# Transposing the query and key stacks by DMA in a token-mixing, attention and expert layer

## The chip, the cores and the metric

The kernel runs on one core of one Trainium2 chip. The metric is the device time of one execution in microseconds. The kernel before took 2010.56 us (median of 3 runs, 2005.82 to 2010.73).

## The reference

The input x has 8 batches of 512 tokens, with 256 entries of 4 taps each. A transformer layer of width 256 follows, all in float32:

```
h = einsum('bhid,oi,od->bho', x, weighted_sum, weight)       # mixing: 1024 inputs to 256
n = layernorm(h)
q, k, v = split(n @ qkv_w.T + qkv_b)                          # 16 heads of 16
q, k = unit(rotate(q)), unit(rotate(k))                       # rotary, then length 1
a = softmax(q @ k.T / 4) @ v                                  # 512 x 512 per head
h = h + a @ out_w.T + out_b
n = layernorm(h)
w = sigmoid(n @ Wg + bg), zero where it is not over 0.5       # 8 experts, dense
h = h + sum_e w[:, e] * (relu(n @ W1[e] + b1[e]) @ W2[e] + b2[e])   # 256 -> 1024 -> 256
```

## The kernel before

**Work.** Every float32 product is made of parts: a high part, and a low part that holds the rest. An expert product is three float16 matmuls (high by high, high by low, low by high). Each batch has 64 chunks (8 experts of 8 hidden tiles of 128). For a chunk, "f1" is the first layer (six matmuls of 512 columns into bank_h, L850), then ScalarE makes two relus of it (L657, float32, and L660, float16 high part), GpSimd makes the low part (L540), and "f2" is the second layer (twelve matmuls of 256 columns into bank_f, L869 to L872), three chunks later. After the eighth chunk of an expert VectorE adds the result to the sum ("acc", L1073), for which the next expert's f2 waits. There are two banks for f1, so TensorE starts f1 of chunk c only when the relus of chunk c - 2 are done.

**Order.** The order of the work is written out by hand. `attention_order()` gives each step of the next batch's mixing and attention a place in units of chunks of this batch's expert work, and `bodies()` merges the two lists into one. Each engine walks through the same merged list, in order, and takes from each step its own part. So what an engine waits for holds up all that stands behind it in the list. A step with a fraction below .5 stands between f1 and f2 of its chunk, otherwise behind f2. The first batch's attention runs alone, in an order of its own (`alone`), with four banks for the scores; there is no expert work beside it. During the experts of batch 0 the float16 parts of the weights are made ("maxima", "scales", "parts") and stored in HBM, later batches load them again.

**Steps of the attention that the change touches.** "split" makes the high part xh (ScalarE) and the low part xl (VectorE) of a tile of x; "mix" is the mixing product of a tile of 128 tokens (L683 to L685); "ln1" the layernorm; "ln1_turn", "qkv" and "rotate" the projection and the rotary step of a tile; "qk_norm 0" and "1" the reciprocal lengths of two tiles; "unit" scales query and key of a tile (L987). "stack" writes both, with their parts, into one float16 buffer `stack`: for the query (high, low, high, low), for the key (high, high, low, low), 16 heads of 64 columns, 1024 in all; ScalarE writes the high half, VectorE the low half (L996). "qk_turn" has TensorE transpose the 2 x 8 blocks of 128 x 128 (L752) into banks bank_s (bank_f in the first batch), and ScalarE copies them to `qt` and `kt`. There is one `stack`, so tile t + 1 waits for the turn of tile t. "scores" need all four tiles of qt and kt. At "qkv 3" GpSimd adds the output bias to the residual (L560).

**SyncE** issues all DMAs, in order, all on one queue. For each expert it waits until the slot is free and loads w1 and w2 (1 MB each). Tile t of x goes into one of two buffers, free when tile t - 2 is split. The result of a batch is stored behind the last expert.

Of the kernel before, what the change touches and what calls it, by code (L numbers as in the profile page):

```python
# [26 lines left out]
P = 128  # L27
# [28 lines left out]
def attention_order(alone=False):  # L56


    steps = []
    for t in range(TT):  # L60
        steps += [(MIX[t - 1] - 0.05 if t else 0.3, "split", t), (MIX[t], "mix", t),
                  (9.0 + 1.5 * t, "ln1_turn", t), (10.55 + 1.5 * t, "qkv", t), (10.6 + 1.5 * t, "rotate", t),
                  (17.1 + 1.5 * t, "unit", t), (18.6 + 1.5 * t, "stack", t), (20 + 1.5 * t, "qk_turn", t)]
    steps += [(6.8, "ln1", 0), (14.7, "qk_norm", 0), (19.2, "qk_norm", 1)]
    if alone:

        order = ["ln1_turn 0", "ln1_turn 1", "qkv 0", "rotate 0", "ln1_turn 2", "qkv 1", "rotate 1", "qk_norm 0",
                 "unit 0", "ln1_turn 3", "qkv 2", "stack 0", "rotate 2", "unit 1", "qkv 3", "qk_turn 0", "stack 1",
                 "rotate 3", "qk_norm 1", "qk_turn 1", "unit 2", "stack 2", "unit 3", "qk_turn 2", "stack 3",
                 "qk_turn 3"]  # L70
        places = {name: 8 + 0.1 * k for k, name in enumerate(order)}
        steps = [(places.get(f"{stage} {n}", at), stage, n) for at, stage, n in steps]
    first = 25.6
    for n in range(2 * UNITS):
        steps.append((first + PACE * n, "scores", n))
    for u in range(UNITS):
        steps.append((first + PACE * (2 * u + 3) + 0.1, "weigh", u))
    for g in range(GROUPS):
        steps += [(first + PACE * (8 * (g + 1) + 1) + 0.15, "out_copy", g),
                  (first + PACE * (8 * (g + 1) + 3) + 0.2, "out_turn", g)]  # L80
    tail = first + PACE * (2 * UNITS + 4) + 1
    for t in range(TT):
        steps += [(tail + t, "att_turn", t), (tail + t + 1.1, "project", t), (tail + 7.6 + 0.8 * t, "ln2_turn", t),
                  (tail + 8.5 + 0.8 * t, "logits", t)]
    steps += [(tail + 5.2, "ln2", 0), (tail + 11.2, "gates", 0), (tail + 12.7, "gates_turn", 0),
              (tail + 13.7, "bias2", 0)]
    steps.sort(key=lambda s: s[0])
    return steps


PACE = 0.66
MIX = [2.1, 3.5, 4.9, 6.3]
PIECES = 4


# [97 lines left out]
def build(nc, x_t, mix_w, mix_sum_t, qkv_w_t, qkv_b, out_w_t, out_b, gate_w, gate_b, w1, b1_t, w2, b2,  # L193
# [5 lines left out]
    with ExitStack() as ctx:  # L199
# [11 lines left out]


        ident = sb("ident", [P, P])
        ident16 = sb("ident16", [P, P], F16)
        mix = sb("mix", [P, 2, XK, D], F32R)
        qkvw = sb("qkvw", [P, 2, DK, QKV], F32R)
        outw = sb("outw", [P, 2, DK, D], F32R)
# [113 lines left out]
        qk_unit = signal("qk_unit", TT)  # L331
        stack_hi = signal("stack_hi", 2 * TT)
        stack_ready = signal("stack_ready", 2 * TT)
        stack_turned = signal("stack_turned", 2 * TT)
        qt_out = signal("qt_out", TT)
        kt_out = signal("kt_out", TT)
        scored = signal("scored", 4 * UNITS)
        exped = signal("exped", 4 * UNITS)
        weighed = signal("weighed", UNITS)
# [36 lines left out]
        def qkv_banks(t, alone):  # L376

            return bank_h if alone and t % 2 else bank_s

        def qk_turn_bank(a, alone):  # L380

            return (bank_f if alone else bank_s)[a][:, :].bitcast(F16).rearrange("p (h t) -> p h t", t=P)

        def stack_slots(t, a):

# [50 lines left out]
        def _(sp):  # L436
# [43 lines left out]
            def load_expert(b, e):  # L480


                s = e % 2
                wait(sp, z_ready, b, HM * (e - 1))
                sp.dma_start(w1s[s][:], w1_parts[e]).then_inc(w1_in[s].sem, 16)
                wait(sp, f2_done, b, HM * (e - 1))
                sp.dma_start(w2s[s][:], w2_parts[e]).then_inc(w2_in[s].sem, 16)

            def store(b):
                for half in range(2):  # L490
# [4 lines left out]

            load_raw(0)
            load_x(1, [0, 1])
            load_raw(1)
            store_parts(0)
            load_x(1, [2, 3])  # L500
            load_raw(2)
            store_parts(1)
            for e in range(2, EXPERTS):
                if e + 1 < EXPERTS:
                    load_raw(e + 1)
                store_parts(e)
# [3 lines left out]
            load_x(2, [0, 1])  # L510
            load_expert(1, 0)
            load_expert(1, 1)
            store(0)

            def body(b, more, far):
                if more:
                    load_x(b + 1, [2, 3])
                for e in range(2, EXPERTS):
                    load_expert(b, e)
                if far:  # L520
                    load_x(b + 2, [0, 1])
                if more:
                    load_expert(b + 1, 0)
                    load_expert(b + 1, 1)
                store(b)

            for i in range(1, BATCHES - 2):
# [6 lines left out]
        def _(pool):  # L534
            def steps(stage, n, fb, ab):
# [15 lines left out]
                elif stage == "reduce":  # L551

                    pool.wait_ge(maxima, 3 * (n + 1))
                    if n:
                        pool.wait_ge(scales, n)
                    pool.partition_all_reduce(mxr[:], mx[:], P, bass.bass_isa.ReduceOp.max).then_inc(maxima_all, 1)
                elif stage == "qkv" and n == TT - 1:

                    wait(pool, ln1_out, ab, TT)
                    pool.tensor_tensor(resid[:], resid[:], outb[:].unsqueeze(1).broadcast_to([P, TT, D]),  # L560
                                       ALU.add).then_inc(resid_biased.sem, 1)
# [1 line left out]
            make_mix(pool, 1)  # L563
            pool.memset(v1[:, :, :, 1, :], 1.0).then_inc(pool_consts, 1)
            pool.wait_ge(consts_in, 16 * 9)
            pool.tensor_copy(ident16[:], ident[:]).then_inc(pool_consts, 1)
            run(pool, steps)

        @block.scalar
        def _(act):  # L570
            def copy(out_ap, in_ap):
                return act.activation(out_ap, in_ap, ACT.Copy)  # L572

            def take_turned(t, a, b, alone):

                dst, done = ((qt, qt_out), (kt, kt_out))[a]
                wait(act, stack_turned, b, 2 * t + a + 1)
                wait(act, scored, b, 0)
                copy(dst[:, :, t * P:(t + 1) * P], qk_turn_bank(a, alone)).then_inc(done.sem, 1)

            def split_x(b, t):

# [6 lines left out]
            def steps(stage, n, fb, ab):  # L589
# [20 lines left out]
                elif stage == "stack":  # L610
                    wait(act, qk_unit, ab, n + 1)
                    for a in range(2):
                        wait(act, stack_turned, ab, 2 * (n - 1) + a + 1)
                        high, _, unit_qk = stack_slots(n, a)
                        copy(high, unit_qk).then_inc(stack_hi.sem, 1)
                        if n:
                            take_turned(n - 1, a, ab, fb is None)
                elif stage == "qk_turn" and n == TT - 1:
                    for a in range(2):
                        take_turned(n, a, ab, fb is None)  # L620
                elif stage == "scores":
                    u, half = divmod(n, 2)
                    if half == 0:
# [53 lines left out]
        def _(pe):  # L677
# [17 lines left out]
            def steps(stage, n, fb, ab):  # L695
# [27 lines left out]
                elif stage == "qkv":  # L723
# [18 lines left out]
                elif stage == "qk_turn":  # L742
                    if fb is not None:
                        wait(pe, qkv_out, ab, 2 * TT)
                    if n == 0 and fb is None:
                        pe.wait_ge(pool_consts, 2)
                    for a in range(2):
                        wait(pe, stack_ready, ab, 2 * n + a + 1)
                        wait(pe, (qt_out, kt_out)[a], ab, n)
                        turned = qk_turn_bank(a, fb is None)  # L750
                        for h in range(HEADS // 2):
                            last = pe.transpose(turned[:, h, :],  # L752
                                                stack[:, a, 2 * h:2 * h + 2, :, :].rearrange("p h s d -> p (h s d)"),
                                                ident16[:])
                        last.then_inc(stack_turned.sem, 1)
                elif stage == "scores":
                    (g, tile), half = divmod(n // 2, TT), n % 2
                    if n == 0:
                        wait(pe, qt_out, ab, TT)
                        wait(pe, kt_out, ab, TT)  # L760
                        wait(pe, qkv_out, ab, 2 * TT)
                    for j in range(2):
                        h = 4 * g + 2 * half + j
# [5 lines left out]
                elif stage == "weigh":  # L769
                    g, tile = divmod(n, TT)  # L770
                    wait(pe, exped, ab, 4 * (n + 1))
                    if n == 0:
                        wait(pe, qkv_out, ab, 2 * TT)
                        wait(pe, ln1_lo, ab, TT)
                    if tile == 0:
                        wait(pe, o_out, ab, g)
                    for j in range(4):
# [103 lines left out]
        def _(dve):  # L881
# [23 lines left out]
            def steps(stage, n, fb, ab):  # L905
# [76 lines left out]
                elif stage == "unit":  # L982

                    wait(dve, weighed, ab, 0)
                    scale = y1[:, n * 2 * HEADS:(n + 1) * 2 * HEADS].unsqueeze(2)\
                        .broadcast_to([P, 2 * HEADS, HD])
                    dve.tensor_tensor(units_at[:, n % 2, :].rearrange("p (h d) -> p h d", d=HD),  # L987
# [2 lines left out]
                elif stage == "stack":  # L990
                    wait(dve, qk_unit, ab, n + 1)
                    for a in range(2):
                        high, low, unit_qk = stack_slots(n, a)
                        wait(dve, stack_hi, ab, 2 * n + a + 1)
                        wait(dve, stack_turned, ab, 2 * (n - 1) + a + 1)
# [182 lines left out]
```

## Time and profile before

| | |
|---|---|
| median of 3 runs | 2010.56 us |
| profiled execution | 2008.53 us, of it span 2006.6 us, mean granted clock 0.975 |
| TensorE busy | 1907.4 us (95%), 13152 matmuls |
| ScalarE, VectorE, GpSimd busy | 57%, 39%, 34% |
| DMA queue of SyncE | 174.52 MB, 24.8% of 16 engines |
| costliest group | L850, first expert layer, 754.8 us in 3072 matmuls |

Starts and durations are in microseconds from the start of the span. The duration of a matmul holds its way through the array: matmuls that follow one another overlap, and what one costs is the distance from its start to the next one's. "[0.40 <-DVE xl]" behind an instruction is the time for which its engine was idle before it and what ended that. PE is TensorE, ACT ScalarE, DVE VectorE, POOL GpSimd, SP SyncE. DMA issues have the time from the issue to the landing.

### The profile page before, as it was taken

How to read it: one execution, taken by the hardware profiler on the slowest of the kernel's cores; microseconds unless marked ns; L12 is line 12 of the kernel's file. 1: busy time of each engine (PE TensorE's matmuls, PEld its weight loads, DVE VectorE, ACT ScalarE, POOL GpSimd, SP SyncE). 2: the span in 40 equal slices, each digit the busy share in tenths (PEclk: the TensorE clock that was granted, in tenths of full speed). 3: DMA queues.
4: the chain of work that ended last, by engine and by line, in shares of the span. 5: the costliest groups of instructions: out<-in, count | busy, mean ns of one | idle time of the engine just before them, and what ended most of it. 6: DMA issues, size and time to landing. Idle time of an engine off the chain costs nothing.

```text
span 2006.6 us, 33214 instructions
## 1 busy us (share of the span) xinstructions
PE 1907.4 (95%) x13152; PEld 1210.5 (60%) x13152; DVE 776.4 (39%) x1636; ACT 1143.0 (57%) x1969; POOL 676.7 (34%) x570
## 2 busy tenths in 40 slices
PE   5679898899999999999999999999999999999999
PEld 4246543576547764577646775467645776466666
DVE  6656933538103470145502372034800455022000
ACT  2654676544774467644765447754576447654444
POOL 1102422335223343333423353233433334233443
PEclk8779999999999999999999999999999999999999
DMA  4013232332112311231212221133211322113221
GB/s 156 31 57 113 104 138 84 126 138 84 64 64 106 115 64 64 79 125 63 83 64 105 97 84 64 64 106 97 83 64 64 124 77 85 64 64 116 101 89 53
DMA packets 40442, 176.64 MB, mean 88 GB/s; under 512 B 4056, under 2 KB 17120, under 8 KB 23904
## 3 DMA queue, kind: packets, MB, share of 16 engines
q1 hardware_dynamic: 40288, 174.52, 24.8%
q8 instruction: 105, 1.72, 0.3%
q14 instruction: 49, 0.40, 0.1%
HBM read 153.54 MB, written 20.97 MB: 87 GB/s over the span
## 4 chain that ended last, share of the span: by engine, by line
PE 78%; DVE 8%; issue 6%; ACT 1%; POOL 1%; POOLq 0%; DVEq 0%; ACTq 0%
PE bank_h L850 28%; PE bank_f L869 10%; PE bank_f L871 10%; PE bank_f L872 10%; PE bank_o L779 5%; PE bank_s L767 3%; PE bank_s L683 2%; PE bank_s L685 2%; PE bank_s L684 2%; PE bank_s L752 1%; DVE qk L972 1%; DVE tmp_b L967 1%; DVE y L890 1%; POOL hl L540 1%; PE bank_s L833 1%
## 5 line engine op out<-in xcount | busy, mean ns | idle before, releaser
L540 POOL TENSOR_TENSOR hl<-h,hh 128x512 f16<-128x512 f32 x512 | 608.2, 1188 | 1131.8 <-ACT hh L660 724.9
L850 PE MATMUL bank_h<-x,w1s 128*128 128x512 f16 x3072 | 754.8, 383 | 9.0 <-ACT hh L660 8.6
L657 ACT ACTIVATE h<-bank_h,b1s 128x512 f32<-128x512 f32 x512 | 353.6, 691 | 453.3 <-PE bank_h L850 438.3
L869 PE MATMUL bank_f<-w2s,hh 128*128 128x256 f16 x2048 | 562.3, 275 | 2.1 <-DVE acc L1073 1.6
L871 PE MATMUL bank_f<-w2s,hh 128*128 128x256 f16 x2048 | 560.5, 274 | 0.0
L872 PE MATMUL bank_f<-w2s,hl 128*128 128x256 f16 x2048 | 560.4, 274 | 0.0
L850 PEld LDWEIGHTS bank_h<-x,w1s 128*128 128x128 f16 x3072 | 288.2, 99 | 333.9 <-issue 43.5
L660 ACT ACTIVATE hh<-bank_h,b1s 128x512 f16<-128x512 f32 x512 | 352.6, 689 | 0.0
L627 ACT ACTIVATE probs<-bank_s 128x512 f32<-128x512 f32 x480 | 262.4, 604 | 154.6 <-PE bank_s L767 154.2
L869 PEld LDWEIGHTS bank_f<-w2s,hh 128*128 128x128 f16 x2048 | 201.9, 99 | 112.5 <-issue 43.0
L1073 DVE SCALAR_TENSOR_TENSOR acc<-bank_f,gw,acc 128x256 f32<-128x256 f32 x256 | 106.1, 477 | 364.0 <-PE bank_f L872 363.9
L871 PEld LDWEIGHTS bank_f<-w2s,hh 128*128 128x128 f16 x2048 | 201.3, 98 | 48.1 <-issue 0.3
L872 PEld LDWEIGHTS bank_f<-w2s,hl 128*128 128x128 f16 x2048 | 201.2, 98 | 24.1
L1000 DVE RECIPROCAL rc<-bank_m 128x16 f32<-128x16 f32 x32 | 8.2, 258 | 400.0 <-PE bank_m L789 400.0
L779 PE MATMUL bank_o<-probs,v 128*32 128x512 f32 x1024 | 138.1, 612 | 1.2 <-ACT tmp_b L572 0.6
L767 PE MATMUL bank_s<-qt,kt 64*128 64x512 f16 x480 | 99.2, 393 | 13.0 <-ACT probs L627 11.8
L683 PE MATMUL bank_s<-mix,xh 128*128 128x256 f32 x256 | 77.9, 304 | 15.9 <-DVE xl L913 15.9
L767 PEld LDWEIGHTS bank_s<-qt,kt 64*128 64x128 f16 x480 | 24.6, 93 | 100.0 <-issue 49.7
L609 ACT ACTIVATE probs<-qk 128x512 f32<-128x512 f32 x32 | 20.2, 630 | 102.9 <-DVE qk L954 102.9
L913 DVE TENSOR_TENSOR xl<-xraw,xh 128x512 fp32r<-128x512 f32 x64 | 47.7, 757 | 76.0 <-ACT xh L572 63.6
L684 PE MATMUL bank_s<-mix,xh 128*128 128x256 f32 x256 | 73.7, 288 | 0.0
L685 PE MATMUL bank_s<-mix,xl 128*128 128x256 f32 x256 | 73.5, 287 | 0.0
(134 smaller groups left out, 1736.0 us busy)
## 6 DMA issues: line engine op xcount, KB each, us to landing
w1s<-w_parts SPq DMA_DIRECT2D x56, 1024.0 KB, 4.8
w2s<-w_parts SPq DMA_DIRECT2D x56, 1024.0 KB, 4.8
xraw<-in_x_t_dram SPq DMA_DIRECT2D x32, 512.0 KB, 4.8
raw<-in_w_dram SPq DMA_DIRECT2D x16, 1024.0 KB, 6.7
w_parts<-w1s SPq DMA_DIRECT2D x8, 1024.0 KB, 8.8
w_parts<-w2s SPq DMA_DIRECT2D x8, 1024.0 KB, 10.7
out_dram<-acc SPq DMA_DIRECT2D x16, 256.0 KB, 6.1
raw<-in_qkv_w_t_dram SPq DMA_DIRECT2D x1, 768.0 KB, 7.2
```

Source lines behind the costliest of these rows:

```text
L540: pool.tensor_tensor(hl[n % HBUFS][:], h32[n % 2][:], hh[n % HBUFS][:], ALU.subtract)\
L627: act.activation(probs[u % 2][:, 2 * half + j, :], score_bank(2 * n + j, fb is None)[:, :], ACT.Exp, scale=SCORE_SCALE).then_inc(exped.sem, 1)
L657: act.activation(h32[n % 2][:], bank_h[n % 2][:, :], ACT.Relu, bias=b1s[:, e, m:m + 1]).then_inc(h_hi.sem, 1)
L660: act.activation(hh[n % HBUFS][:], bank_h[n % 2][:, :], ACT.Relu, bias=b1s[:, e, m:m + 1]).then_inc(h_hi.sem, 1)
L683: pe.matmul(out_ap, high[k], w[k], start=start and k == 0, stop=False, skip_group_check=True)
L684: pe.matmul(out_ap, high[k], lo_w[k], start=False, stop=False, skip_group_check=True)
L767: pe.matmul(score_bank(2 * n + j, fb is None)[:, :], kt[lo:lo + 64, h // 2, tile * P:(tile + 1) * P], qt[lo:lo + 64, h // 2, :], start=Tru ...
L779: last = pe.matmul(bank_o[32 * j:32 * j + 32, :], v1[:, tile, h, :, :].rearrange("p s d -> p (s d)"), probs[n % 2][:, j, :], start=(tile = ...
L850: last = pe.matmul(bank_h[n % 2][:, :], w[:, wp, k, m * P:(m + 1) * P], x16s[fb % 2][:, xp, k, :], start=(k == 0 and wp + xp == 0), stop=( ...
L869: pe.matmul(o, high, w[:, 0, m, :], start=(m == 0 and t % 2 == 0), stop=False, skip_group_check=True)
L871: pe.matmul(o, high, w[:, 1, m, :], start=False, stop=False, skip_group_check=True)
L872: last = pe.matmul(o, low, w[:, 0, m, :], start=False, stop=(m == HM - 1), skip_group_check=True)
```

## The change

TensorE's transposes of the stacks, their banks' use, ScalarE's copies to qt and kt and the step "qk_turn" are gone. SyncE issues two transposing DMAs per tile instead (`turn_stacks`), each 128 x 1024 in float16, from `stack` to the tile's columns of qt or kt. ScalarE's and VectorE's parts of "stack" now wait for the landing of the tile before; "scores" wait for the landing of all. The places move: mixing, layernorm and projection come 1.1 chunks earlier, unit 0 is at 15.2 instead of 17.1, and units 1 to 3 at 17.9, 19.2 and 20.5 instead of 18.6, 20.1 and 21.6; each stack is 1.4 behind its unit. Scores begin at 25.6 as before. The output bias is added at 23.7. On SyncE, the first tile's transposes stand between the loads of w1 and w2 of expert 3, the others behind them; tiles 2 and 3 of x are asked for before the store of the batch instead of behind it.

```
-                  (9.0 + 1.5 * t, "ln1_turn", t), (10.55 + 1.5 * t, "qkv", t), (10.6 + 1.5 * t, "rotate", t),
-                  (17.1 + 1.5 * t, "unit", t), (18.6 + 1.5 * t, "stack", t), (20 + 1.5 * t, "qk_turn", t)]
-    steps += [(6.8, "ln1", 0), (14.7, "qk_norm", 0), (19.2, "qk_norm", 1)]
+                  (7.9 + 1.5 * t, "ln1_turn", t), (9.45 + 1.5 * t, "qkv", t), (9.5 + 1.5 * t, "rotate", t),
+                  (UNIT[t], "unit", t), (UNIT[t] + 1.4, "stack", t)]
+    steps += [(5.7, "ln1", 0), (12.9, "qk_norm", 0), (15.7, "qk_norm", 1), (23.7, "out_bias", 0)]
...
-MIX = [2.1, 3.5, 4.9, 6.3]
+MIX = [1.0, 2.4, 3.8, 5.2]
+UNIT = [15.2, 17.9, 19.2, 20.5]
...
                 sp.dma_start(w1s[s][:], w1_parts[e]).then_inc(w1_in[s].sem, 16)
+                if e == 3 and b + 1 < BATCHES:
+                    turn_stacks(b + 1, [0])
                 wait(sp, f2_done, b, HM * (e - 1))
                 sp.dma_start(w2s[s][:], w2_parts[e]).then_inc(w2_in[s].sem, 16)
+            def turn_stacks(b, tiles):
+                for t in tiles:
+                    for a in range(2):
+                        wait(sp, stack_ready, b, 2 * t + a + 1)
+                        if t == 0:
+                            wait(sp, scored, b, 0)
+                        sp.dma_start_transpose((qt, kt)[a][:, :, t * P:(t + 1) * P],
+                                               stack[:, a].rearrange("p h s d -> p (h s d)"))\
+                          .then_inc(stack_turned[a].sem, 16)
...
             load_x(1, [0, 1])
+            turn_stacks(0, range(TT))
             load_raw(1)
...
             for e in range(2, EXPERTS):
+                if e == 3:
+                    turn_stacks(1, range(TT))
                 if e + 1 < EXPERTS:
                     load_raw(e + 1)
...
             def body(b, more, far):
-                if more:
-                    load_x(b + 1, [2, 3])
                 for e in range(2, EXPERTS):
                     load_expert(b, e)
+                    if more and e == 3:
+                        turn_stacks(b + 1, range(1, TT))
                 if far:
                     load_x(b + 2, [0, 1])
                 if more:
                     load_expert(b + 1, 0)
                     load_expert(b + 1, 1)
+                if far:
+                    load_x(b + 2, [2, 3])
                 store(b)
...
-                elif stage == "qkv" and n == TT - 1:
+                elif stage == "out_bias":
...
                 elif stage == "stack":
                     wait(act, qk_unit, ab, n + 1)
                     for a in range(2):
-                        wait(act, stack_turned, ab, 2 * (n - 1) + a + 1)
+                        wait(act, stack_turned[a], ab, 16 * n)
                         high, _, unit_qk = stack_slots(n, a)
                         copy(high, unit_qk).then_inc(stack_hi.sem, 1)
-                        if n:
-                            take_turned(n - 1, a, ab, fb is None)
...
                     if n == 0:
-                        wait(pe, qt_out, ab, TT)
-                        wait(pe, kt_out, ab, TT)
+                        for turned in stack_turned:
+                            wait(pe, turned, ab, 16 * TT)
                         wait(pe, qkv_out, ab, 2 * TT)
```

## Rows read from the trace of the kernel before

**Rows 1.** Page, first part: busy time and share of the span of each engine.
```profile
PE 1907.4 (95%) x13152; PEld 1210.5 (60%) x13152; DVE 776.4 (39%) x1636; ACT 1143.0 (57%) x1969; POOL 676.7 (34%) x570
```

**Rows 2.** Stretches by window: one steady batch; columns named in the first line.
```profile
core 0: us, PE busy (x) PEld busy (x) DVE busy (x) ACT busy (x) POOL busy (x), PEclk, DMA share, GB/s
660.00:895.00 235.00, 233.06 (x1647) 148.23 (x1645) 86.07 (x187) 138.50 (x242) 83.22 (x69) 1.00 0.24 84
```

**Rows 3.** Groups by line and shape, as in the page's part 5.
```profile
L657 ACT ACTIVATE h<-bank_h,b1s 128x512 f32<-128x512 f32 x512 | 353.6, 691 | 453.3 <-PE bank_h L850 438.3 <-POOL hl L540 14.3
...
L752 PE MATMUL bank_s<-ident,stack 128*128 128x128 f16 x448 | 32.2, 222 | 6.3 <-issue 4.4 <-DVE stack L996 1.5
L572 ACT ACTIVATE stack<-probs 128x512 f16<-128x512 f32 x64 | 39.8, 634 | 32.9 <-DVE probs L987 32.9
...
L572 ACT ACTIVATE qt<-bank_s 128x1024 f16<-128x1024 f16 x28 | 29.2, 1043 | 0.0
...
L752 PE MATMUL bank_f<-ident,stack 128*128 128x128 f16 x64 | 7.2, 286 | 13.4 <-ACT qt L572 7.1 <-DVE stack L996 5.5 <-ACT kt L572 0.8
```

**Rows 4.** Timeline of PE, 494 to 520 us: start, duration, line, operation, count.
```profile
498.18 1.06 PE L752 MATMUL bank_s<-ident,stack 128*128 128x128 f16 x16
499.07 0.27 PE L869 MATMUL bank_f<-w2s,hh 128*128 128x256 f16 x1
...
503.37 1.18 PE L752 MATMUL bank_s<-ident,stack 128*128 128x128 f16 x16 [0.22 <-issue]
504.39 1.46 PE L850 MATMUL bank_h<-x,w1s 128*128 128x512 f16 x6
...
506.99 1.46 PE L850 MATMUL bank_h<-x,w1s 128*128 128x512 f16 x6
508.29 1.06 PE L752 MATMUL bank_s<-ident,stack 128*128 128x128 f16 x16
509.18 0.27 PE L869 MATMUL bank_f<-w2s,hh 128*128 128x256 f16 x1
...
513.10 1.29 PE L752 MATMUL bank_s<-ident,stack 128*128 128x128 f16 x16
514.23 1.46 PE L850 MATMUL bank_h<-x,w1s 128*128 128x512 f16 x6
```

**Rows 5.** Timelines of POOL, ACT and PE, 484 to 492 us.
```profile
484.19 2.35 POOL L560 TENSOR_TENSOR resid<-resid,outb 128x1024 f32<-128x1024 f32 x1
...
489.46 0.63 ACT L609 ACTIVATE probs<-qk 128x512 f32<-128x512 f32 x1 [6.47 <-DVE qk L954]
...
491.30 1.04 PE L850 MATMUL bank_h<-x,w1s 128*128 128x512 f16 x4 [0.97 <-ACT hh L660]
```

**Rows 6.** Timelines of PE, ACT and DVE at the start of a batch.
```profile
660.52 4.29 PE L850 MATMUL bank_h<-x,w1s 128*128 128x512 f16 x18
665.21 0.36 PE L683 MATMUL bank_s<-mix,xh 128*128 128x256 f32 x1 [0.40 <-DVE xl L913]
...
663.17 1.15 ACT L572 ACTIVATE xh<-xraw 128x512 fp32r<-128x512 f32 x2
...
663.89 1.78 DVE L913 TENSOR_TENSOR xl<-xraw,xh 128x512 fp32r<-128x512 f32 x2 [2.07 <-issue]
```

**Rows 7.** Page, part 6: DMA issues, KB each, us from issue to landing.
```profile
w1s<-w_parts SPq DMA_DIRECT2D x56, 1024.0 KB, 4.8
...
out_dram<-acc SPq DMA_DIRECT2D x16, 256.0 KB, 6.1
...
raw<-in_mix_sum_t_dram SPq DMA_DIRECT2D x1, 256.0 KB, 2.9
```

**Rows 8.** Timelines of ACT and DVE, first batch, stacks 2 and 3.
```profile
68.31 0.63 ACT L572 ACTIVATE stack<-probs 128x512 f16<-128x512 f32 x1 [5.35 <-DVE probs L987]
...
75.89 1.02 ACT L572 ACTIVATE kt<-bank_f 128x1024 f16<-128x1024 f16 x1 [0.28 <-PE bank_f L752]
...
69.02 0.69 DVE L996 TENSOR_TENSOR stack<-probs,stack 128x512 f16<-128x512 f32 x1 [0.75 <-ACT stack L572]
```

More of the change, by code:

```diff
@@ L61, in attention_order @@
         steps += [(MIX[t - 1] - 0.05 if t else 0.3, "split", t), (MIX[t], "mix", t),
-                  (9.0 + 1.5 * t, "ln1_turn", t), (10.55 + 1.5 * t, "qkv", t), (10.6 + 1.5 * t, "rotate", t),
-                  (17.1 + 1.5 * t, "unit", t), (18.6 + 1.5 * t, "stack", t), (20 + 1.5 * t, "qk_turn", t)]
-    steps += [(6.8, "ln1", 0), (14.7, "qk_norm", 0), (19.2, "qk_norm", 1)]
+                  (7.9 + 1.5 * t, "ln1_turn", t), (9.45 + 1.5 * t, "qkv", t), (9.5 + 1.5 * t, "rotate", t),
+                  (UNIT[t], "unit", t), (UNIT[t] + 1.4, "stack", t)]
+    steps += [(5.7, "ln1", 0), (12.9, "qk_norm", 0), (15.7, "qk_norm", 1), (23.7, "out_bias", 0)]
     if alone:
         order = ["ln1_turn 0", "ln1_turn 1", "qkv 0", "rotate 0", "ln1_turn 2", "qkv 1", "rotate 1", "qk_norm 0",
-                 "unit 0", "ln1_turn 3", "qkv 2", "stack 0", "rotate 2", "unit 1", "qkv 3", "qk_turn 0", "stack 1",
-                 "rotate 3", "qk_norm 1", "qk_turn 1", "unit 2", "stack 2", "unit 3", "qk_turn 2", "stack 3",
-                 "qk_turn 3"]
+                 "unit 0", "ln1_turn 3", "qkv 2", "stack 0", "rotate 2", "unit 1", "qkv 3", "stack 1",
+                 "rotate 3", "qk_norm 1", "unit 2", "stack 2", "unit 3", "stack 3"]
         places = {name: 8 + 0.1 * k for k, name in enumerate(order)}
@@ L213, in build @@
         ident = sb("ident", [P, P])
-        ident16 = sb("ident16", [P, P], F16)
         mix = sb("mix", [P, 2, XK, D], F32R)
@@ L333, in build @@
         stack_ready = signal("stack_ready", 2 * TT)
-        stack_turned = signal("stack_turned", 2 * TT)
-        qt_out = signal("qt_out", TT)
-        kt_out = signal("kt_out", TT)
+        stack_turned = [signal(f"stack_turned{a}", 16 * TT) for a in range(2)]
         scored = signal("scored", 4 * UNITS)
@@ L378, in qkv_banks @@
             return bank_h if alone and t % 2 else bank_s
-        def qk_turn_bank(a, alone):
-            return (bank_f if alone else bank_s)[a][:, :].bitcast(F16).rearrange("p (h t) -> p h t", t=P)
         def stack_slots(t, a):
@@ L512, in _ @@
             load_expert(1, 1)
+            load_x(2, [2, 3])
             store(0)
             def body(b, more, far):
-                if more:
-                    load_x(b + 1, [2, 3])
                 for e in range(2, EXPERTS):
                     load_expert(b, e)
+                    if more and e == 3:
+                        turn_stacks(b + 1, range(1, TT))
                 if far:
@@ L565, in _ @@
             pool.wait_ge(consts_in, 16 * 9)
-            pool.tensor_copy(ident16[:], ident[:]).then_inc(pool_consts, 1)
             run(pool, steps)
@@ L572, in copy @@
                 return act.activation(out_ap, in_ap, ACT.Copy)
[L574 to L579, printed above, removed]
             def split_x(b, t):
@@ L612, in steps @@
                     for a in range(2):
-                        wait(act, stack_turned, ab, 2 * (n - 1) + a + 1)
+                        wait(act, stack_turned[a], ab, 16 * n)
                         high, _, unit_qk = stack_slots(n, a)
                         copy(high, unit_qk).then_inc(stack_hi.sem, 1)
-                        if n:
-                            take_turned(n - 1, a, ab, fb is None)
-                elif stage == "qk_turn" and n == TT - 1:
-                    for a in range(2):
-                        take_turned(n, a, ab, fb is None)
                 elif stage == "scores":
@@ L741, in steps @@
                     last.then_inc(qkv_done.sem, 1)
[L742 to L755, printed above, removed]
                 elif stage == "scores":
@@ L774, in steps @@
                         wait(pe, ln1_lo, ab, TT)
+                        if fb is None:
+                            pe.wait_ge(pool_consts, 1)
                     if tile == 0:
@@ L984, in steps @@
                     wait(dve, weighed, ab, 0)
+                    if n >= 2:
+                        wait(dve, stack_ready, ab, 2 * (n - 1))
                     scale = y1[:, n * 2 * HEADS:(n + 1) * 2 * HEADS].unsqueeze(2)\
@@ L994, in steps @@
                         wait(dve, stack_hi, ab, 2 * n + a + 1)
-                        wait(dve, stack_turned, ab, 2 * (n - 1) + a + 1)
+                        wait(dve, stack_turned[a], ab, 16 * n)
                         dve.tensor_tensor(low, unit_qk, high, ALU.subtract).then_inc(stack_ready.sem, 1)
```

## The prediction

> **What bounds the kernel now.** I read the page's engine shares first: TensorE is busy for 95% of the span [rows 1]. The stretches by window come second: one steady batch, from one first-layer start to the next, lasts 235.0 us, TensorE is busy in 233.1 of them, at a granted clock of 1.00 (2.4 GHz), while ScalarE is at 138 and VectorE at 86 [rows 2]. So in six of the eight periods time is TensorE's work plus its few idle gaps, and what the other engines save is worth nothing unless it closes a gap. The timelines come last, for the places where the change acts: the four transposing groups [rows 4], the one gap that ScalarE causes before them [rows 5], the start of a batch [rows 6], and the first batch's attention, which has no expert work beside it and is a chain of latencies [rows 8].
>
> **Term 1, the transposes leave TensorE.** 448 of the 512 are in the merged batches [rows 3], 64 in each of seven. Means of overlapping matmuls (222 ns) are no price; start to start is. The four groups of 16 hold TensorE from 498.18 to 499.07, 503.37 to 504.39, 508.29 to 509.18 and 513.10 to 514.23 [rows 4]: 0.89 + 1.02 + 0.89 + 1.13 = 3.93 us per batch. All of it is on the saturated engine: **-3.93 us**. ScalarE also loses eight copies of 1.04 us per batch [rows 3]; they end no TensorE wait, so I count them at nothing by themselves.
>
> **Term 2, the residual bias leaves the norm.** In the batch before, GpSimd's addition of the output bias (2.35 us, at 484.19) lies beside the first qk_norm on VectorE; the third qkv result comes late, ScalarE waits 6.47 us for it at 489.46, its two relus come late, and TensorE idles 0.97 us at 491.30 [rows 5]. Now the addition comes at 23.7, where VectorE has nothing urgent, and qk_norm 0 stands 1.05 chunks before qkv 3 instead of 0.35. **-0.97 us**. If the cover fails (the same stall in qk_norm 1), the term is 0.
>
> **Term 3, mix 0 moves ahead of the third first-layer group.** MIX[0] goes from 2.1 to 1.0, so mix 0 follows f1 chunk 1 instead of chunk 2. At the start of the batch shown, three f1 groups run from 660.52 and mix 0 starts at 665.21, 0.40 us late, for xl [rows 6]. A group is half of a chunk of 506.99 - 504.39 = 2.60 us [rows 4], so f1 chunk 1 ends at 660.52 + 2.6 = 663.1. The first half of xl is written from 663.89, half of 1.78 us, so it is there at 664.8 [rows 6]; nothing makes it earlier, since ScalarE's xh stands behind its first relu as before (663.17). TensorE now waits 1.6 us there instead of 0.4: **+1.2 us**. Between 0 (if the relus slip behind) and 1.6. Tiles 2 and 3 of x are still asked for as soon as tile 0 and 1 are split; one that lands in 4.8 us is in time, and the store, which now stands behind these waits on SyncE's queue, holds a buffer that is not needed for forty chunks. Both cost nothing.
>
> **Term 4, the waits that come in.** The stack is one buffer, so ScalarE's high half of tile t+1 now waits until the DMA has landed tile t, and behind that high half the relus of the expert layer are queued, for which TensorE waits. Call l the time from a stack half being ready to its transpose being seen landed. The trace has none. Nearest rows: a 256 KB load in 2.9 us, below which I find nothing of this size; a 1 MB load in 4.8; a 256 KB store in 1 KB rows in 6.1 [rows 7]. Ends: 2.4 (no HBM in it) and 6.1; a slower one is a rival. I take 3.2, the 256 KB load and a little.
>
> Set T = 0 at f1 chunk 16, chunks of 2.6 us. w2 of expert 3 is asked for at f2 chunk 15's end, T = 7.8, and done at 12.6; it is on the same queue. Stack 0 (place 16.6) is turned by T = 8 to 9. Stack 1 (19.3): ScalarE's relus of chunk 19 end at 10.4, high halves take 0.63 and 0.5 more, low halves 0.69 and 0.6 [rows 3, 8]: ready at 11.8 and 12.4, landed at 11.8 + l and 12.4 + l. Stack 2 (20.6) may start at 13.0 but waits. For l = 3.2: high halves end at 15.6 and 16.2, relus of chunk 21 (1.3 us, [rows 3]) at 17.5. TensorE's f1 chunk 23 wants them at 18.2: no loss. Stack 2 is ready at 16.3 and 16.9, landed at 19.5 and 20.1. Stack 3 (21.9) is written by 20.7, relus of chunk 22 end at 22.0, wanted at 20.8: 1.2 us lost. Scores begin at T = 25, and stack 3 lands at 21.5 + 3.2: in time. The same steps give 0 at l = 2.6, 0.6 at 2.9, 2.8 at 4 and 8.0 at 6 (there the scores wait as well); about two waits count, so 2 us per us of l. **+1.2 us**, between 0 and 8.
>
> **Sum per merged batch:** -3.93 - 0.97 + 1.2 + 1.2 = -2.5 us. Seven batches have it; six at 235 us and the one during batch 0's experts, which is looser, and for which I take the same: -17.5 us.
>
> **Term 5, the first batch's attention, alone.** Here each DMA is on the path. Stack 2's high halves start at 68.31, its first low half at 69.02; the last copy of kt ends at 75.89 + 1.02 = 76.9 and the scores follow [rows 8]. Now both high halves run at once, the low halves are ready at 69.7 and 70.3, landed at 72.9 and 73.5; stack 3 is ready at 74.2 and 74.9 and landed at 78.1: +1.2 us, in general 2(l - 2.6). The four turns of TensorE and the kt and qt copies there are inside this comparison. TensorE then sits idle for the whole stretch, so the first scores may run at the lower level; the scores there are paced by ScalarE's exponentials, so I add nothing.
>
> **Total:** 2008.53 - 17.5 + 1.2 = 1992.2 us for the profiled execution. That was 2.0 us below the median of the runs shown, 2010.56; I say 1993. SyncE's other queue entries (raw weights and parts of the first batch) stand at times later than the stacks in the code's places: load_raw(1) and load_raw(4) wait for parts that are made after the last stack is ready, so nothing is late behind the new waits. Nothing of GpSimd's queue gets longer.
>
> **A rule of the skill, beside term 4.** The bound here is by rows 7, a plain 256 KB load at 2.9 us. The Trainium skill (DMA: Bandwidth & Descriptors, Latency and other measured facts) gives a DMA transpose an effective 261 GB/s, so an estimate by that page is 1.0 us of data for 256 KB on top of the fixed part. Against it the Trainium skill (Advanced Engine Details and Errata, DGE: Hardware vs Software) calls the transposing efficiency of the hardware generator, which SyncE uses, the worse of the two. By the first the sum stays near mine; by the second it is rival B. No row here can say which.
>
> **Rivals.**
> A. *Forecast*, l between 2.7 and 3.9 and the rest as above: 1985 to 2000. Chance 0.45.
> B. *The transpose is slow, slower than before.* It breaks even where term 4 eats the rest: -3.7 + 2(l - 2.6) = 0, l about 4.5. At l = 6, near the store's 6.1, a merged batch costs 8.0 - 3.7 = +4.3 us, seven +30, the front +7: 2045. For it: small pieces are what a transposed write must consist of, and the only row with 1 KB pieces is the slow one; two of the eight can also meet the 1 MB load on the queue. Against it: the DMA engines are busy for 24% only [rows 2], and that store ends in HBM. The place is ScalarE's high half of stacks 2 and 3. Chance 0.34.
> C. *Clean gain*: l at most 2.6, and mix 0 finds its xl. Per batch -3.93 - 0.97 + 0.4 = -4.5 and the front 0: 1977. For it: no HBM. Against: 2.9 is the least seen. Chance 0.15.
> D. *The gain is given back*: stalls of terms 3 and 4 take all of terms 1 and 2 (l of 4.2 to 4.7): 2004 to 2014. Chance 0.06.
>
> **How the numbers follow.** A measurement of this kernel tells about 0.3%, 6 us, from no change. Faster: A and C, 0.60. Same: D, 0.06. Slower: B, 0.34. The forecast's own range is 1985 to 2000. The range for 8 in 10 takes in C's end and B up to a little over l = 6: 1976 to 2052. What is left out is mostly l well above 6, where a pair of transposes takes longer than two chunks.
>
> **What would show it.** Term 1: no group with the stack as input on TensorE, and chunks 19 to 23 of 2.60 us. Term 2: no TensorE gap behind qkv 3. Term 3: a gap of about 1.6 us before mix 0 in each batch. Term 4: the landing time of the transposing DMAs, ScalarE waiting for them at stacks 2 and 3 and not at 1, and a TensorE gap of about 1 us at f1 chunk 24. The steady period should be 232.5 us. Term 5: the first scores at about 78 us instead of 77.0. I am wrong if the landing is over 4 us, or if TensorE waits for the first scores of a merged batch.

## The result and the profile after

The changed kernel takes 2027.01 us (median of 5 runs, 2023.42 to 2029.34) against 2010.56 us (now 5 runs too, 2005.82 to 2016.69, with the same median): ratio 1.0074, 95% interval 1.0057 to 1.0092. It is slower by some 15 us by the ratio, where 1993 us were forecast. The profiled execution took 2027.32 us, 18.8 us more than that of before. Starts of the experts' first chunk in each batch (the first L850 / L837 group of each) split this up: +2.4 us lie before batch 0's experts, +5.7 us in the first period (297.5 instead of 291.8 us), and +10.8 us in the six merged periods behind it, which take 235.7 to 238.2 us instead of 235.0. Inside a merged period, chunks 32 to 63 take the same time as before, and so does the last batch (170.8 us); the difference lies in chunks 0 to 31.

The page after: busy time, the queue, and the two groups whose idle time (behind the second bar) grew; then the landing times of the new DMAs, and one steady period by window.

```profile
PE 1882.9 (93%) x12640; PEld 1187.8 (59%) x12640; DVE 744.0 (37%) x1636; ACT 1089.3 (54%) x1905; POOL 674.6 (33%) x569
...
q1 hardware_dynamic: 107872, 191.31, 28.8%
...
L856 PE MATMUL bank_f<-w2s,hh 128*128 128x256 f16 x2048 | 565.9, 276 | 25.3 <-DVE acc L1062 25.1
...
L682 PE MATMUL bank_s<-mix,xh 128*128 128x256 f32 x256 | 80.3, 314 | 28.9 <-DVE xl L900 27.8
```

```profile
qt<-stack SPq DMA_TRANSPOSE x32, 2.7
kt<-stack SPq DMA_TRANSPOSE x32, 2.8
```

```profile
core 0: us, PE busy (x) PEld busy (x) DVE busy (x) ACT busy (x) POOL busy (x), PEclk, DMA share, GB/s
1144.60:1381.30 236.70, 230.25 (x1582) 145.40 (x1580) 80.87 (x188) 131.94 (x234) 82.89 (x69) 0.99 0.29 92
```

TensorE is busy for 2.8 us less in the period than in [rows 2], 230.25 instead of 233.06 us, and yet the period is longer. f2 (L856) idles 25.3 us, nearly all of it for VectorE's expert sum (acc); before, the group's idle time was 2.1 us. The mixing product idles 28.9 us instead of 15.9. The transposes themselves land in 2.7 to 2.8 us.

**Ahead of mix 0**, PE and DVE, the answer to [rows 6]:

```profile
908.85 2.75 PE L837 MATMUL bank_h<-x,w1s 128*128 128x512 f16 x12
913.53 0.36 PE L682 MATMUL bank_s<-mix,xh 128*128 128x256 f32 x1 [1.93 <-DVE xl L900]
...
912.21 1.77 DVE L900 TENSOR_TENSOR xl<-xraw,xh 128x512 fp32r<-128x512 f32 x2 [2.06 <-issue]
```

Two f1 groups instead of three, then a gap of 1.93 us instead of 0.40.

**At the expert sum**, DVE and PE. In the kernel before, VectorE makes the sum behind unit 0 and ahead of stack 0, and TensorE waits 0.16 us:

```profile
494.52 1.65 DVE L1073 SCALAR_TENSOR_TENSOR acc<-bank_f,gw,acc 128x256 f32<-128x256 f32 x4
...
495.53 0.27 PE L869 MATMUL bank_f<-w2s,hh 128*128 128x256 f16 x1 [0.16 <-DVE acc L1073]
```

In the changed kernel:

```profile
971.58 0.67 DVE L960 TENSOR_REDUCE ss<-probs 128x32 f32<-128x512 f32 x1
972.17 0.68 DVE L976 TENSOR_TENSOR probs<-qk,y 128x512 f32<-128x512 f32 x1
972.77 1.15 DVE L967 TENSOR_SCALAR ss<-ss 128x64 f32<-128x64 f32 x1
...
977.58 2.25 DVE L985 TENSOR_TENSOR stack<-probs,stack 128x512 f16<-128x512 f32 x2
979.75 0.68 DVE L976 TENSOR_TENSOR probs<-qk,y 128x512 f32<-128x512 f32 x1
980.36 1.65 DVE L1062 SCALAR_TENSOR_TENSOR acc<-bank_f,gw,acc 128x256 f32<-128x256 f32 x4
...
981.37 0.27 PE L856 MATMUL bank_f<-w2s,hh 128*128 128x256 f16 x1 [2.48 <-DVE acc L1062]
...
983.49 2.31 PE L837 MATMUL bank_h<-x,w1s 128*128 128x512 f16 x6
985.64 0.27 PE L856 MATMUL bank_f<-w2s,hh 128*128 128x256 f16 x1
```

VectorE does the rotary step of tile 3, unit 0 (972.17), the chain of qk_norm 1 (972.77 to 977.58), stack 0 and unit 1, and only then the sum of expert 1 (980.36). The f2 of the next expert waits for it, 2.48 us. What follows runs slowly: the f1 group that starts at 983.49 is done at 985.64, 2.15 us instead of 1.30. The granted clock of the stretches, as columns in [rows 2]:

```profile
976.00:979.00 3.00, 2.88 (x20) 1.67 (x17) 2.83 (x7) 1.34 (x3) 1.76 (x2) 1.00 0.00 0
...
982.00:985.60 3.60, 3.60 (x14) 1.82 (x13) 2.59 (x5) 0.63 (x1) 0.00 (x0) 0.55 0.75 252
```

Behind the gap 3.4 us pass at half clock (1.2 GHz), and so it is in five of the six batches. In the merged batches before there was no such stretch.

**On SyncE's queue**, with ScalarE's high halves and TensorE:

```profile
978.30 1.24 SPq L491 DMA_TRANSPOSE qt<-stack  x1
979.86 1.23 SPq L491 DMA_TRANSPOSE kt<-stack  x1
981.14 0.57 SPq L482 DMA_DIRECT2D w2s<-w_parts  x1
983.23 1.24 SPq L491 DMA_TRANSPOSE qt<-stack  x1
984.51 2.65 SPq L491 DMA_TRANSPOSE kt<-stack  x1
989.80 1.23 SPq L491 DMA_TRANSPOSE qt<-stack  x1
...
981.13 0.63 ACT L583 ACTIVATE stack<-probs 128x512 f16<-128x512 f32 x1 [0.94 <-DMA qt<-stack]
...
988.37 0.63 ACT L583 ACTIVATE stack<-probs 128x512 f16<-128x512 f32 x1 [1.25 <-DMA qt<-stack]
...
992.59 0.63 ACT L583 ACTIVATE stack<-probs 128x512 f16<-128x512 f32 x1 [1.60 <-DMA qt<-stack]
...
995.83 1.46 PE L837 MATMUL bank_h<-x,w1s 128*128 128x512 f16 x6 [0.90 <-ACT hh L659]
```

The load of w2 (981.14) stands behind the transposes of stack 0, and the transposes of stack 1 then stand behind its 1 MB. They land 5.1 and 4.7 us after their issue, and ScalarE goes on with the high half of stack 2 at 988.37; the first one of stack 2 needs 2.7 us (ScalarE goes on at 992.59). Over the six batches the first half of stack 1, issued 2.1 us behind the load each time, lands after 4.8 to 7.6 us. ScalarE's relus stand behind the high halves, and TensorE waits 0.90 us at 995.83. These gaps, at f1 chunks 23 and 24, come to 0.6 to 3.4 us per batch, 1.8 us in the mean.

### The profile page after: what moved, and what is told of

Its sections match the earlier page's. It is cut to its first block, busy times and chain, and to the rows that moved or that the text cites. A ratio compares the mean times of both kernels' runs of the same rounds, so it can differ in the third digit from the quotient of the medians.

```text
span 2025.5 us, 32101 instructions
## 1 busy us (share of the span) xinstructions
PE 1882.9 (93%) x12640; PEld 1187.8 (59%) x12640; DVE 744.0 (37%) x1636; ACT 1089.3 (54%) x1905; POOL 674.6 (33%) x569
## 4 chain that ended last, share of the span: by engine, by line
PE 73%; DVE 7%; issue 7%; DMA 3%; ACT 2%; POOL 2%; SPq 0%; DVEq 0%; POOLq 0%; ACTq 0%
PE bank_h L837 27%; PE bank_f L856 10%; PE bank_f L858 9%; PE bank_f L859 9%; PE bank_o L766 5%; DMA kt<-stack 3%; PE bank_s L752 3%; PE bank_s L682 3%; PE bank_s L684 2%; PE bank_s L683 2%; POOL hl L552 1%; DVE stack L985 1%; PE bank_s L820 1%; PE bank_m L776 1%; DVE qk L959 1%
## 5 line engine op out<-in xcount | busy, mean ns | idle before, releaser
L837 PE MATMUL bank_h<-x,w1s 128*128 128x512 f16 x3072 | 756.1, 383 | 12.8 <-ACT hh L659 12.8
L856 PE MATMUL bank_f<-w2s,hh 128*128 128x256 f16 x2048 | 565.9, 276 | 25.3 <-DVE acc L1062 25.1
L837 PEld LDWEIGHTS bank_h<-x,w1s 128*128 128x128 f16 x3072 | 289.7, 99 | 336.8 <-issue 56.2
L856 PEld LDWEIGHTS bank_f<-w2s,hh 128*128 128x128 f16 x2048 | 202.9, 99 | 139.5 <-issue 69.3
L682 PE MATMUL bank_s<-mix,xh 128*128 128x256 f32 x256 | 80.3, 314 | 28.9 <-DVE xl L900 27.8
L752 PEld LDWEIGHTS bank_s<-qt,kt 64*128 64x128 f16 x480 | 24.0, 93 | 121.5 <-issue 69.7
L583 ACT ACTIVATE stack<-probs 128x512 f16<-128x512 f32 x64 | 39.3, 628 | 72.6 <-DMA qt<-stack 30.4
L985 DVE TENSOR_TENSOR stack<-probs,stack 128x512 f16<-128x512 f32 x64 | 55.7, 887 | 55.6 <-ACT stack L583 54.7
L683 PE MATMUL bank_s<-mix,xh 128*128 128x256 f32 x256 | 76.0, 297 | 0.0
```

Of the source, the lines that this page charges most:

```text
L682: pe.matmul(out_ap, high[k], w[k], start=start and k == 0, stop=False, skip_group_check=True)
L683: pe.matmul(out_ap, high[k], lo_w[k], start=False, stop=False, skip_group_check=True)
L752: pe.matmul(score_bank(2 * n + j, fb is None)[:, :], kt[lo:lo + 64, h // 2, tile * P:(tile + 1) * P], qt[lo:lo + 64, h // 2, :], start=Tru ...
L837: last = pe.matmul(bank_h[n % 2][:, :], w[:, wp, k, m * P:(m + 1) * P], x16s[fb % 2][:, xp, k, :], start=(k == 0 and wp + xp == 0), stop=( ...
L856: pe.matmul(o, high, w[:, 0, m, :], start=(m == 0 and t % 2 == 0), stop=False, skip_group_check=True)
```

## The experiments

Each was timed in alternation with the kernel before; the ratio is to that kernel.

**Only the DMA turn (e5).** The changed kernel with all places of before.

```
-MIX = [1.0, 2.4, 3.8, 5.2]        UNIT = [15.2, 17.9, 19.2, 20.5]; stack at UNIT + 1.4
+MIX = [2.1, 3.5, 4.9, 6.3]        UNIT = [17.1, 18.6, 20.1, 21.6]; stack at UNIT + 1.5
+ln1 6.8; ln1_turn 9.0, qkv 10.55, rotate 10.6 (+ 1.5 t); qk_norm 14.7 and 19.2; out_bias 15.06
```

> The changed kernel with every place of the kernel before (mixing, norms, units, stacks, output bias); only TensorE's transposes are replaced by DMAs. Theory P (the moved places cost more than the DMA gives): about 3.9 us less TensorE work per batch, no 2.5 us wait for the expert sum and no clock drop, part of it lost because stack 1 to 3 still land behind a 1 MB load: 1990 to 2008. Rival D (the DMA turn itself is what costs): still slower than before, 2020 or more.

2016.04 us, 1.0022 (1.0011 to 1.0032). Neither theory's range: two thirds of what the changed kernel lost comes back, but nothing is won. The gap of 0.97 us behind qkv 3 is still there, and there is a new one of 1.9 to 3.1 us before f1 chunk 24, with 0.5 to 1.6 us more before the scores in four of the six batches.

**Only the places (e6).** The kernel before with the places of the changed one; TensorE transposes at 18.0, 20.55, 21.85 and 23.3. Units 2 and 3 also wait on VectorE for the stack two before them, as in the changed kernel.

> The kernel before with the places of the changed one; TensorE still transposes. Theory P: the 1.9 us gap ahead of mix 0 and the 2.5 us gap for the expert sum with its stretch at half clock appear in every merged batch, without any DMA transpose: 1.5 + 2.5 + 1.7 - 1.0 = 4.7 us per batch, about 2035 to 2045. Rival D: the gaps come with the DMA waits; then this one is within 0.3% of before, 2004 to 2016.

2044.33 us, 1.0159 (1.0138 to 1.0179), in the range of theory P: the moved places alone cost 32 us against before, and the DMA turn takes 17 us of these off again. DVE and PE of this kernel:

```profile
742.80 2.25 DVE L1000 TENSOR_TENSOR stack<-probs,stack 128x512 f16<-128x512 f32 x2
...
743.59 0.61 PE L754 MATMUL bank_s<-ident,stack 128*128 128x128 f16 x8 [2.10 <-issue]
745.11 0.62 PE L754 MATMUL bank_s<-ident,stack 128*128 128x128 f16 x8 [0.91 <-DVE stack L1000]
...
747.66 2.34 PE L852 MATMUL bank_h<-x,w1s 128*128 128x512 f16 x6
```

There is no DMA turn here, and VectorE still writes stack 0's low half only at 742.80, behind qk_norm 1. TensorE stands at the transposes, 2.10 and 0.91 us, and the f1 group behind runs at half clock. VectorE is late in the same way as in the changed kernel, and the transposes meet it instead of the sum. The gap of 1.93 us ahead of mix 0 is there too, in all six batches. So the places lose more than the whole 15 us, without any DMA turn. How the changed kernel's own loss is made up does not follow from this run, since its stalls lie elsewhere.

**Mix 0 back behind the third f1 (e1).**

```
-MIX = [1.0, 2.4, 3.8, 5.2]
+MIX = [2.1, 3.1, 4.2, 5.2]
```

> The changed kernel with the mixes at 2.1, 3.1, 4.2 and 5.2 chunks instead of 1.0, 2.4, 3.8 and 5.2. Theory P: the gap ahead of mix 0 goes from 1.93 to about 0.4 us, seven times, and the half-clock stretches behind it in two batches go: 10 to 14 us less than the changed kernel, 2013 to 2017. Rival: the relus behind the splits are late instead and the time stays at 2027.

2012.51 us, 1.0002 (0.9992 to 1.0013), 14.5 us less than the changed kernel, a little more than theory P had. Chunks 0 to 7 take 29.5 us instead of 30.7 to 32.3 us, and the period of batch 0's experts 294.1 instead of 297.5 us.

**qk_norm 1 behind the expert sum (e2).**

```
-(15.7, "qk_norm", 1)     UNIT = [15.2, 17.9, 19.2, 20.5]
+(19.0, "qk_norm", 1)     UNIT = [15.2, 17.4, 20.6, 21.9]     # stack at UNIT + 1.4
```

> The changed kernel with qk_norm 1 at 19.0 instead of 15.7, behind the expert sum at 18.5, and units at 15.2, 17.4, 20.6, 21.9. Theory P: VectorE reaches the sum in time, the 2.48 us gap and the 3.4 us at half clock behind it go (4.2 us per batch), and stack 2 no longer waits for the landing of stack 1: 1998 to 2008. Rival D: the DMA waits of stacks 1 to 3 hold the relus all the same, and the scores wait at the end: 2020 or more.

2031.65 us, 1.0092 (1.0072 to 1.0112). The time is where rival D had it, and the scores do wait at the end, as D said; but theory P is right at the place of the edit: chunks 16 to 23 take 20.8 us, which is TensorE without a gap (26.0 to 28.7 after), but chunks 24 to 31 take 32.3 to 35.8 us instead of 29.2. ACT, SP and PE of this kernel:

```profile
753.86 1.15 ACT L583 ACTIVATE stack<-probs 128x512 f16<-128x512 f32 x2
...
758.59 0.63 ACT L583 ACTIVATE stack<-probs 128x512 f16<-128x512 f32 x1 [2.02 <-DMA qt<-stack]
...
760.69 1.23 SPq L491 DMA_TRANSPOSE qt<-stack  x1
761.97 1.31 SPq L491 DMA_TRANSPOSE kt<-stack  x1
...
764.84 0.61 PE L752 MATMUL bank_s<-qt,kt 64*128 64x512 f16 x2 [3.05 <-issue]
```

Stack 2 is written at 753.86 although its unit was done before 751.9, stack 3 is turned too late, and the scores wait 3.05 us for it (3.1 to 4.2 us over the six batches), here again with half clock behind. The wait was not removed but moved. Two things hold stack 2: its place (22.0), and stack 1, whose halves are issued behind the load of w2 here too and land only at 751.8 and 752.6. This run does not separate them.

**w2 behind all transposes (e3).**

```
-turn_stacks(b + 1, [0]) between w1 and w2 of expert 3, the others behind w2
+turn_stacks(b + 1, range(TT)) between w1 and w2 of expert 3
```

> The changed kernel with all four tiles' transposes ahead of the load of w2 of expert 3 on SyncE. Theory Q (the 1 MB load issued between stacks 0 and 1 delays the landing of stack 1 from 2.7 to about 5 us): stack 1 lands in 2.8 us, ScalarE's relus are in time and the 0.6 to 3.4 us of gaps at chunks 22 to 24 go, 8 to 12 us in all: 2014 to 2019. The 2.5 us gap for the expert sum stays. Rival: stack 2 and 3 are late by VectorE and not by the queue; the time stays at 2025 or more.

2018.39 us, 1.0040 (1.0023 to 1.0057): 7 to 9 us less than the changed kernel (by the ratios and by the medians), where theory Q had 8 to 12. The first half of stack 1 now lands in 2.7 us in five of the six batches, instead of 4.8 to 7.6 us. The periods are 234.7 to 236.6 us; the gap for the expert sum stays at 2.48 us.

**The same order of loads with the old places (e9).**

> The kernel with the old places and the DMA turns (2016 when it was run), with all transposes ahead of the load of w2. Theory Q: the 2 to 2.8 us gap at chunk 24 and the half-clock stretch behind it go, about 3.5 us per batch: 1988 to 1996, faster than before. Rival: TensorE waits there for the stacks whatever the queue holds: 2010 or more.

2012.56 us, 1.0022 (1.0009 to 1.0035), the ratio of e5. Theory Q fails here, and its rival (2010 or more) holds: the load was not what stacks 2 and 3 waited for. PE:

```profile
748.00 1.46 PE L835 MATMUL bank_h<-x,w1s 128*128 128x512 f16 x6 [1.86 <-ACT hh L657]
...
755.00 0.39 PE L750 MATMUL bank_s<-qt,kt 64*128 64x512 f16 x2 [1.63 <-issue]
```

With the old places stack 3 stands at 23.1, and a turn that needs 2.7 us to land, behind 1.3 us for the kt half, is not done when the scores are due: relus 1.86 us late at chunk 24, scores 1.63 us late at 755.00. With the DMA turn the stacks have to stand earlier; in e7 below the last one is at 22.7.

**And the output bias late (e8).**

```
-(15.06, "out_bias", 0)
+(23.7, "out_bias", 0)
```

> The same, with the output bias added at 23.7 instead of 15.06. Theory of the prediction's second term: the 0.97 us gap at chunk 18 goes in seven batches, 6 to 7 us less than the run without it: 1982 to 1989. Rival: the first qk_norm is slow by itself and the gap stays; same time as the run without it.

2019.13 us, 1.0048 (1.0030 to 1.0066), 6.6 us more than without it. The gap behind qkv 3 (0.96 us here) is gone in all six batches, as the prediction's second term says, and chunks 16 to 23 fall from 24.4 to 22.8 us, but chunks 24 to 31 rise from 30.9 to 33.9 us. POOL and DVE:

```profile
752.71 2.81 POOL L570 TENSOR_TENSOR resid<-resid,outb 128x1024 f32<-128x1024 f32 x1
...
753.86 2.21 DVE L983 TENSOR_TENSOR stack<-probs,stack 128x512 f16<-128x512 f32 x1 [0.56 <-ACT stack L581]
```

Here the addition on GpSimd lies beside the low half of stack 3, which takes 2.21 us instead of 0.69; it is the same meeting as in [rows 5], at a worse place.

**All three moves (e7, and e12 once more).** Mixes as in e1, w2 as in e3, and stacks that do not wait for their place:

```
-(15.7, "qk_norm", 1)     UNIT = [15.2, 17.9, 19.2, 20.5]     stack at UNIT + 1.4
+(19.0, "qk_norm", 1)     UNIT = [15.2, 17.4, 20.6, 21.2]     STACK = [16.6, 18.8, 21.4, 22.7]
```

> The changed kernel with the mixes at 2.1, 3.1, 4.2, 5.2, qk_norm 1 at 19.0, units at 15.2, 17.4, 20.6, 21.2, stacks at 16.6, 18.8, 21.4, 22.7, and w2 of expert 3 behind all transposes. If the three causes (mix 0, the expert sum, the load) are all there is, a merged batch takes 235.0 - 3.9 - 1.0 = 230 us: 1978 to 1988. If scores still wait for stack 3: about 2000.

> The three moves once more, on the chip of the two others, for the comparison: 1980 to 1988 by either theory.

1983.42 us, 0.9880 (0.9856 to 0.9904), and 1981.96 us, 0.9861 (0.9837 to 0.9884): both in the expected range, and faster than both kernels. A steady period of e12:

```profile
662.30:891.80 229.50, 228.70 (x1582) 144.91 (x1580) 80.38 (x188) 131.81 (x234) 82.96 (x69) 1.00 0.30 95
```

Five of the six merged periods of e12 take 229.5 to 229.6 us (three in e7); TensorE is busy for 228.70 us of the one shown. The others take 231.0 to 231.5 us and lose the rest at chunk 25, where TensorE waits for relus or scores. No stretch of the merged batches runs at half clock. How much the move of qk_norm 1 gives by itself no run shows: by the ratios all moves give 39 to 43 us, of which e1 alone gave 14.5 and e3 alone 7 to 9; if the parts add up, an estimate of some 20 us is left for qk_norm 1 and the stacks' places.

**The same places, TensorE transposing (e11).**

> The kernel before (TensorE transposes and ScalarE copies) with the places of the three moves. It gives the worth of the DMA turn at equal places: by the removed work 3.9 us per merged batch, so 233 us per batch instead of 229.5 and 2005 to 2012 in all. Rival: with the gaps gone TensorE has room for the transposes and the time is within 6 us of the DMA version's 1983; or the copies make ScalarE late and it is over 2015.

2000.02 us, 0.9947 (0.9929 to 0.9965), between the two expected ranges; the period is as expected:

```profile
665.80:898.60 232.80, 232.27 (x1647) 148.59 (x1646) 80.80 (x188) 138.58 (x242) 82.68 (x69) 1.00 0.24 84
```

232.8 us per period against 229.5. So at equal places the DMA turn is worth 3.3 us per batch and 18 us in all; the places alone are worth 11 us.

**Raw weights ahead of stack 3 (e10),** in batch 0's experts, on top of e7.

> The kernel with the three moves (1983 when it was run), with the load of raw w1 of expert 4 ahead of stack 3's transposes during batch 0's experts, instead of behind all of them. Theory S (the first expert period is 298 us instead of 292 because the raw loads stand behind the stacks on SyncE, 254 instead of 240 us): 3 to 6 us less, 1978 to 1981. Rival: that period is long because of VectorE and ScalarE; then within 2 us of the run without it.

1983.48 us, 0.9869 (0.9847 to 0.9891), the same as e12 within the noise. The load goes out earlier, at 248.38 instead of 254 us in e7 and 251.9 in e12, and the first period is 297.8 us, against 298.0 and 296.0 in those two, which are one kernel:

```profile
248.38 0.58 SPq L461 DMA_DIRECT2D raw<-in_w_dram  x1
```

Theory S is wrong. e11 and e6, without any DMA turn, have 298 us there too, and e5 and e9, with the old places, 294. So the new places can cost 4 us without a DMA turn; but e1, with most of them, has 294.1 as well, and e8, with only the bias moved, 296.7. In which step the time goes was not settled.

## Why the prediction was wrong

The profiled executions differ by +18.8 us, where the sum had -16.3. Of these 35 us, 26 lie in the six merged periods (+1.8 us each instead of -2.5), 8 in the period of batch 0's experts (+5.7 instead of -2.5) and 1 ahead of it. (The last step of the sum is off by 1 us: 1992.2 + 2.0 is 1994, not 1993.)

**Term 1 (-3.93 us per batch): right in kind, 3.3 us by e11 against e12.** Chunk by chunk the first three groups of transposes cost 0.9, 0.9 and 1.0 us. The fourth costs 0.5 us: in the chunk where it stood, e12 waits for ScalarE's relus, 0.27 us in the period shown.

**Term 2 (-0.97 us): right.** The gap behind qkv 3 is gone in the changed kernel. That at 23.7 "VectorE has nothing urgent" is false for e8, where stack 3 is written there; the changed kernel writes it earlier. Together terms 1 and 2 were priced at 4.9 us; chunks 16 to 31 of e12 take 50.5 us against 56.0 before, 5.5 us less, with the new places.

**Term 3 (+1.2 us): the right wait, too small.** The gap is 1.93 - 0.40 = 1.5 us longer. The sum let mix 0 start when the first half of xl is written; it starts 0.43 us later (913.53, against 912.21 and half of 1.77), and so it did before (665.21). The clock came on top: in two of the six batches a half-clock stretch of 3.4 us follows, so that chunks 0 to 7 take 31.3 us in the mean against 29.3: +2.0 us.

**Term 4 (+1.2 us): near in size, with half of the mechanism.** I took l = 3.2 us; on a free queue the runs show 2.7, and by my own steps that is a loss of 0.2. But I let w2 be asked for at T = 7.8 and be done at 12.6, put no price on a transpose that stands behind it, and counted SyncE's own time for a transpose at nothing. That time is 1.23 us each, the second one 1.3 us behind the first. In the batch shown (T = 0 at 969.61) stack 0 is written late, behind qk_norm 1, so it has landed at T = 13.0 and not at 8 to 9; w2 goes out behind its transposes at T = 11.5, 2.1 us before stack 1's, and is done at 17.7. Stack 1 then lands after 4.8 to 7.6 us over the six batches, and the gaps come to 1.8 us per batch in the mean. The prediction's own sign of being wrong, a landing over 4 us, came at this stack.

**The step that failed is one that the sum does not have.** The prediction prices moved places by TensorE alone. qk_norm 1 moved from 19.2, behind the sum of expert 1 (18.5), to 15.7, ahead of it, and so the 4.8 us of its chain and stack 0 and unit 1 now stand ahead of the sum on VectorE. The prediction names this step once, "If the cover fails (the same stall in qk_norm 1), the term is 0", and so only as a saving that might not come; its own cost has no term. It costs 2.48 us of waiting and, in five of six batches, 1.7 us by the half clock (3.4 us at half speed), 3.9 us in the mean. e2 shows that the place of qk_norm 1 is the cause: with it behind the sum the gap is gone in all six batches, and chunks 16 to 23 take 20.8 us. Term by term: -3.93 - 0.97 + 2.0 + 1.8 + 3.9 = +2.8 us; measured are +1.8 in the mean of six. Of the 1.0 us between them, 0.6 is in terms 1 and 2 (5.5 instead of 4.9) and 0.2 in chunks 8 to 15 (30.0 instead of 30.2).

**The period of batch 0's experts (-2.5 us): +5.7 us.** The sum took it to be like the merged ones. It lost in chunks 8 to 15 (36.9 to 39.9 us), in chunks 56 to 63 (33.2 to 36.0) and in chunks 0 to 7 (40.1 to 42.8). e11, without a DMA turn, has 40.3 and 36.1 in the first two, and 38.3 in the third. Why remains open.

**Term 5 (+1.2 us): +2.4 us.** SP and PE of the changed kernel, the answer to [rows 8]:

```profile
75.28 1.23 SPq L491 DMA_TRANSPOSE qt<-stack  x1
76.56 1.31 SPq L491 DMA_TRANSPOSE kt<-stack  x1
...
79.46 0.61 PE L752 MATMUL bank_s<-qt,kt 64*128 64x512 f16 x2 [22.41 <-DMA kt<-stack]
```

The last half is issued at 76.56 and the scores start at 79.46, 2.9 us later; before they started at 77.0. I had the halves ready 0.6 us apart; SyncE's issue makes that 1.28, once per stack. That offsets the shorter landing, by luck: from stack 2's first issue (71.03) to the last landing 8.3 us pass, and I had 8.4 (69.7 to 78.1). The other half of the 2.4 us was there before stack 2, whose first half was to be ready at 69.7. The loads at the start differ by 3 us between the two executions; that part is not separated from the change.

**Rivals.** B came out in sign and for the smaller part in mechanism: it asks for l over 4.5 at every stack, and l is 2.7 at all but those that meet a load. Its aside, that two of the eight can meet the 1 MB load, is what happened at stack 1, and its place, ScalarE's high halves of stacks 2 and 3, accounts for 1.8 us per batch. The measured 2027 us lies in the prediction's wide range (1976 to 2052) only because that range took in B; that is luck, since the largest part of the loss is in a step that no rival names.

The Trainium skill's figure (DMA: Bandwidth & Descriptors, Latency and other measured facts) gave an estimate of 1.0 us of data; the 2.7 us that were measured leave 1.7 us for the fixed part, which no run here measures apart. The Trainium skill (Advanced Engine Details and Errata, DGE: Hardware vs Software) calls the hardware generator's transposing efficiency the worse; no run here has a transpose by the other one. What the runs show, and I did not price, is SyncE's own time: 1.23 us for one transpose, against 0.32 us for a plain 1 MB load at its shortest.

## What to carry to other kernels

When steps of a hand-written order are moved, walk every engine's queue past them, not only the busiest engine's: ask what now stands ahead of an instruction for which the busy engine waits (here the expert sum behind a 5 us chain on VectorE), and price the clock behind the gap with the gap. A DMA that replaces work of a full engine pays (3.3 us per batch here) only when its source is ready early enough and no large load stands before it on its queue. Removing one of several waits in a chain can show no gain, as in e2; the three moves together gave 39 to 43 us against the changed kernel.

## What the runs showed of the hardware

- A transposing DMA of 128 x 1024 float16 from SBUF to SBUF lands 2.7 to 2.8 us after its issue when the queue is free and takes SyncE 1.23 us to issue. Issued 2.1 us behind a 1 MB load it lands after 4.8 to 7.6 us in six batches of the changed kernel, and SyncE is held for 2.3 to 3.7 us by the one behind it. With the load behind it (e3) it lands after 2.7 us in five of six.
- In the changed kernel's merged batches TensorE runs at 2.4 GHz but for seven stretches of 3.4 us at 1.2 GHz. Five of them follow the six gaps of 2.48 us for the expert sum, two the six gaps of 1.93 us ahead of mix 0, and none the gaps of 0.64 to 2.1 us at chunks 23 and 24, nor those of 0.97 us in the kernel before. The length of the gap alone does not decide: behind the same gap of 1.93 us there are four stretches in six batches in e3, and five in e2 and in e6.
